# Loading q and k into attention: one transfer per half of a row block, over 128 partitions, in place of one per token half, over 64

## What is computed

```python
xn = _layernorm(x)
# graph part: mean over incoming edges of edge_attr (106250 edges, sorted by dst), then an MLP
agg = segment_sum(edge_attr, dst) / max(count, 1)
g   = xn + relu(concat([xn, agg]) @ W1 + b1) @ W2 + b2
# attention part: 8 heads of 64, q and k through a sigmoid, flow normalizers over all tokens
q, k, v = split(xn @ W_qkv.T + b_qkv)          # q, k = sigmoid(q), sigmoid(k)
i, o, i_hat, o_hat = ...                       # sums of q and k over the tokens
vw = v * softmax(o_hat, over tokens)
kv = einsum('bshd,bshe->bsde', k, vw)          # per token: 64 x 64, summed over the 8 heads
r  = einsum('bshd,bsde->bshe', q / i, kv) * sigmoid(i_hat)
x  = x + g + r.reshape(...) @ W_out.T + b_out
# expert part: one expert for all tokens, picked from their mean
x  = x + gate * (layernorm(x) @ We[idx] + be[idx])
```

## Time and profile before

| | |
|---|---|
| median of 3 runs | 2133.06 us (2132.67 to 2135.23) |
| the profiled execution, its own time | 2125.06 us |
| its span, first to last instruction | 2123.3 us |
| PE busy / mean granted clock | 89% / 0.920 |
| POOL, DVE, ACT busy | 63%, 58%, 26% |
| DMA: packets, bytes, mean rate | 502384, 400.77 MB, 189 GB/s |
| hardware queue 1 / software queue 0, share of the 16 engines | 60.2% / 21.8% |
| attention: first load issued, last matmul begins | 1096.93 us, 1575.84 us |

### The profile page before, as it was taken

How to read it: one execution, slowest core, us unless ns; L and a number is a source line. 1 busy time by engine, 2 the same in 40 slices (tenths; PEclk the granted TensorE clock), 3 DMA queues, 4 the chain that set the end, 5 groups by cost and what they waited for, 6 DMA issues and landing times. The chain is left out here.

```text
span 2123.3 us, 31099 instructions
## 1 busy us (share of the span) xinstructions
PE 1884.5 (89%) x10776; PEld 1515.4 (71%) x10776; DVE 1226.6 (58%) x3872; ACT 561.9 (26%) x1314; POOL 1330.5 (63%) x850
## 2 busy tenths in 40 slices
PE   2799999999999999788776989889867999998798
PEld 1688888888888888544435767767755888886686
DVE  3644453443543432277845656666648888885575
ACT  1422333223332223111122121222223434333210
POOL 4888888888888888688888878887886000000100
PEclk9999999999999999866596898989888999999899
DMA  9977887777787777798699999999969776653884
GB/s 286 227 152 146 149 164 149 157 148 139 156 157 152 138 138 138 183 233 204 143 313 184 213 186 218 184 215 194 209 130 249 220 216 209 211 182 118 299 292 151
DMA packets 502384, 400.77 MB, mean 189 GB/s; under 512 B 356932, under 2 KB 369476, under 8 KB 502228
## 3 DMA queue, kind: packets, MB, share of 16 engines
q1 hardware_dynamic: 380164, 369.74, 60.2%
q0 software_dynamic: 119952, 28.99, 21.8%
q10 hardware_dynamic: 2112, 0.07, 0.1%
HBM read 244.05 MB, written 154.62 MB: 188 GB/s over the span
## 5 line engine op out<-in xcount | busy, mean ns | idle before, releaser
L297 POOL DMA_INDIRECT table<-edge_ring,edge_row x831 | 1318.7, 1587 | 305.8 <-issue 228.6
L237 DVE SCALAR_TENSOR_TENSOR edge_sel<-edge_dst_all,edge_dst_f,upper 128x128 f32<-128x128 int16 x831 | 318.0, 439 | 92.7 <-PE edge_sum L249 74.6
L365 PE MATMUL pr_out_bank<-pr_norm_xT_hi,pr_w_hi 128*128 128x512 f32 (+1 forms) x832 | 327.5, 394 | 0.0
L249 PEld LDWEIGHTS edge_sum<-edge_attr,edge_sel 128*128 128x128 f32 x1662 | 241.0, 216 | 109.8 <-DVE edge_sel L237 78.9
L365 PE MATMUL pr_out_bank<-pr_norm_xT_lo,pr_w_hi 128*128 128x512 f32 (+1 forms) x832 | 319.3, 384 | 0.0
L365 PE MATMUL pr_out_bank<-pr_norm_xT_hi,pr_w_lo 128*128 128x512 f32 (+1 forms) x832 | 318.5, 383 | 0.0
L249 PE MATMUL edge_sum<-edge_attr,edge_sel 128*128 128x65 f32 x1662 | 251.5, 301 | 71.1 <-DVE edge_sel L237 70.5
L262 ACT ACTIVATE edge_ring<-edge_sum 128x260 f32<-128x260 f32 (+1 forms) x209 | 80.6, 386 | 561.0 <-PE edge_sum L249 489.0
L2289 POOL DMA_INDIRECT ex_w_raw<-in_w_exp,ex_row x4 | 5.9, 1486 | 335.6 <-issue 335.6
L365 PEld LDWEIGHTS pr_out_bank<-pr_norm_xT_lo,pr_w_hi 128*128 128x128 f32 x832 | 156.6, 188 | 32.1
L365 PEld LDWEIGHTS pr_out_bank<-pr_norm_xT_hi,pr_w_lo 128*128 128x128 f32 x832 | 157.1, 189 | 28.3
(11 more groups left out here) (206 smaller groups left out, 3220.8 us busy)
## 6 DMA issues: line engine op xcount, KB each, us to landing
edge_dst_all<-dst SPq DMA_DIRECT2D x103, 256.0 KB
edge_attr<-in_edge_attr SPq DMA_DIRECT2D x103, 256.0 KB
qk_halves<-pr_stage SPq DMA_DIRECT2D x48, 512.0 KB
h_pre_T<-pr_stage SPq DMA_DIRECT2D x48, 512.0 KB
gn_pre<-h_pre_T SPq DMA_DIRECT2D x48, 512.0 KB, 6.7
done<-qk_halves SPq DMA_DIRECT2D x16, 1024.0 KB
table<-edge_ring,edge_row POOLq DMA_INDIRECT x831
pr_norm_x<-in_x SPq DMA_DIRECT2D x12, 1024.0 KB
```

The lines of the kernel that those rows point to most:

```text
L237: op = dve.scalar_tensor_tensor(out=self.sel[q][0:rows, j, 0:rows], in0=self.dst_all[k][0:rows, t:t + m * (rows - 1) + 1:m], scalar=self.d ...
L249: mm = pe.matmul(self.p_sum[q][0:rows, j * ECOLS:(j + 1) * ECOLS], self.sel[q][0:rows, j, 0:rows], self.attr[k][0:rows, j0 + j, :], start= ...
L297: pool.indirect_dma_start(self.c.table[t], bass.IndirectOffsetOnAxis(ap=self.row[k][0:rows, j:j + 1], axis=0), self.sums[k][0:rows, j, :], ...
L365: mm = pe.matmul(out, a, c, start=first and i == 0, stop=last and i == n - 1)
```

## The change

`load_qk` still issues four transfers for a block. In a full block each now brings the even or the odd heads of one side for both token halves: 128 partitions, on each one run of 4 KB, again 512 KB. The destination's first dimension is the 128 partitions; the source's dimensions are the two token halves, 64 rows, and the run. The order of the four goes from q, k, q, k to q, q, k, k. In the tail block the four transfers have the shapes and the order that they had. Waits and semaphores are the same.

```diff
         def load_qk(b):
-            for half, r in enumerate([BT // 2, BT // 2] if b < FULL else [TAIL]):
-                for side, dst in enumerate((q[b % 2], kk[b % 2])):
-                    rows = slice(half * HDIM, (half + 1) * HDIM)
-                    if r == HALF:
-                        sp.dma_start(dst[rows, :, :].rearrange("d (x o) t -> d x (o t)", x=2),
-                                     c.qk[side, 2 * b + half, :, :, :].rearrange("(x d) o t -> d x (o t)", x=2)
+            for side, dst in enumerate((q[b % 2], kk[b % 2])):
+                for x in range(2):
+                    rows, chunks = slice(x * HDIM, (x + 1) * HDIM), slice(x * CH, (x + 1) * CH)
+                    if b < FULL:
+                        sp.dma_start(dst[:, chunks, :].rearrange("p o t -> p (o t)"),
+                                     c.qk[side, 2 * b:2 * b + 2, rows, :, :].rearrange("w d o t -> w d (o t)")
                                      ).then_inc(qk_in[b % 2], 16)
                     else:
-                        for x in range(2):
-                            sp.dma_start(dst[rows, x * CH:(x + 1) * CH, 0:r],
-                                         c.qk[side, 2 * b, x * HDIM:(x + 1) * HDIM, :, 0:r]).then_inc(qk_in[b % 2], 16)
+                        sp.dma_start(dst[0:HDIM, chunks, 0:TAIL],
+                                     c.qk[side, 2 * b, rows, :, 0:TAIL]).then_inc(qk_in[b % 2], 16)
```

## The result

| | kernel before | changed kernel |
|---|---|---|
| median | 2132.86 us (2128.69 to 2135.23, 4 runs) | 2529.47 us (2523.39 to 2534.71, 4 runs) |
| profiled execution, its own time | 2125.06 us | 2529.68 us |
| its span | 2123.3 us | 2527.9 us |
| ratio, 95% interval | | 1.1863 [1.1834, 1.1892] |

The changed kernel is 19% slower. In the profiled executions the difference is 404.6 us.

The account below looks back on a forecast made before the run. Attention's blocks were taken to end on DMA transfers, largely q and k. +32 at the start, +312 over 11 blocks and 0 behind gave +344 on 2125.06: 2469, or 2477 as median, range 2390 to 2629.

Parts of the forecast that it names:

- Two engines, the same two: Attention's q and k loads: all four confined to the same two DMA engines by the outermost count of 2; chance 0.82.
- A block of 65 us: Period of a full attention block on two engines: 65 us, the middle of 60 to 71, against 36.6 before.
- a rest: Attention block's time beyond q and k: an average engine's other work, queued on the two engines, 18 to 28.6 us.
- the 42 us for q and k: Time two engines at 25 GB/s each take to move a block's 2.1 MB of q and k.
- Issues cost about 0.6 us each before and after: SyncE's issues of transfers in attention: claimed to cost about 0.6 us each, unchanged by the change.
- The start, +32: Block 0's q and k land 42 - 9.5 = 32 us later on two engines, delaying the start of attention.
- The tail, 0: After attention's last load: compute as before, scatters keep up, GNN start unchanged; 0, at best a few us won.
- 312: Loads for blocks 1 to 11 set attention's pace: 11 x (65 - 36.6) = +312 us.
- Sixteen engines: Rival for the q and k loads: engine count follows SBUF's 128; -35 us, 2098, from 2080 to 2118; chance 0.12.
- Others for each load: Rival: each q and k load gets a different two engines; 2133 to 2145 us; 0.06 together with the no-effect rival.
- doesn't do what it says: Rival: q and k's load rate comes from scatters, not partitions; 2133 us; 0.06 together with the different-engines rival.

Follow-up runs that it names:

- reordered features: Against the changed kernel: q and k features interleaved by head parity when weights are loaded, so 128 rows stand first on both sides; 2081.04 us, ratio 0.9781 to the kernel before.
- 57 rows and 7: Kernel before, each full-block q and k load of 64 rows cut into one of 57 rows and one of 7; 2356.38 us, ratio 1.105.
- 62 rows and 2: Kernel before, each full-block q and k load of 64 rows cut into one of 62 rows and one of 2; 2559.68 us, ratio 1.2046.
- block 0 alone: Kernel before with only block 0's q and k loads in the changed form, all later ones as before; 2157.37 us, ratio 1.0136.

## Why the prediction was right, and what was off

One table over all kernels that change the number of engines, from the trace's packets: q and k of a block from first to last packet (mean of 11 blocks), first packet to first packet of the next (mean of 10), and the difference.

| kernel | engines | q, k in flight, us | block, us | rest, us |
|---|---|---|---|---|
| before | 16 | 11.9 | 37.1 | 25.2 |
| reordered features | 16 | 7.8 | 32.9 | 25.1 |
| q alone changed | 2, 16 | 31.2 | 54.4 | 23.2 |
| 57 rows and 7 | 3 | 32.9 | 55.8 | 22.9 |
| changed | 2 | 46.8 | 70.1 | 23.3 |
| changed, no scatters | 2 | 42.8 | 64.7 | 21.9 |
| 62 rows and 2 | 2 | 49.9 | 73.0 | 23.1 |

**Two engines, the same two.** Right, and shown three ways: the share of 0.13 at 51 GB/s, the 62-row kernel that loses 20% with nothing but its count, and the three-engine kernel between. That all four loads share their engines is in the times too: a load's 128 packets on two engines of its own take 64 x 183 ns = 11.7 us, and q and k were in flight for 46.8, four times that; in the first 20 us of the block shown, with both loads of q issued before them, 1.8 packets are in flight in the mean, not four. And of v's load, which goes to all 16, just 128 of 1024 packets are held back until k has ended: two sixteenths. By the Trainium skill ("DMA: Bandwidth & Descriptors", Why a DMA increments its semaphore by 16) the largest number up to 16 that divides the outermost counts of both sides decides. The runs agree: 2 and 128 gives two engines, 62 gives two, and 57 gives 1.105, which lies where three engines put it.

**A block of 65 us.** The block is q and k's time and a rest, as forecast, and the rest measured 23.3; it stayed between 21.9 and 25.2 in every kernel. That 23 was hit is in part luck, see below. The term that was mis-sized is the 42 us for q and k: I took 25 GB/s an engine over the 22 of the 106-row store, and measured 46.8 us. The 25 is right for engines that have nothing else, 51 GB/s in the stretch above; what I put into the rest alone, and not into q and k's time, is that the scatters' packets take their turns on the same two engines. Without them it was 42.8. The 4.8 us a block, times 11, are 53 us of the miss.

**The rest is not made of what I made it of.** I had v, the mixing rows and the edge loads queue on the two engines, and priced that as an average engine's other work, 18 to 28.6 us. The order is right, as v's last 128 packets and the mixing rows behind them show. But the DMA share is 0.68 in the rest, so an average engine works 15.1 of its 22.28 us (the trace doesn't show the two by themselves); and leaving out the scatters, 10.5 us of that work, took 1.4 us from it. What the prediction had wrong is SyncE: "Issues cost about 0.6 us each before and after". The four issues of q and k hold it for 25.0 us a block (4.5 before), v's for 10.6, the first of the mixing rows' for 16.1 (13.1 before), and in the trace SyncE waits for no other engine for more than 0.3 us in all of these blocks, before or after: its issues follow one on the other (held 354.9 of 368.5 us before, 683.6 of 699.9 after). The means of ten blocks:

| us from one event to the next | before | changed | no scatters |
|---|---|---|---|
| first to last packet of q and k | 12.0 | 46.8 | 42.8 |
| to the end of the mixing rows' first issue | 3.5 | 2.9 | 2.9 |
| to the next block's first issue for q (all other issues) | 16.8 | 15.5 | 14.9 |
| to its first packet | 4.8 | 4.8 | 4.1 |

So the rest is what SyncE has to issue between two blocks' loads, about the same whatever q and k take (with the reordered features alone SyncE waits for PE in it), and a block is q and k's time on their engines plus that. This is read from the traces; no run moved the issues to another queue, and that a full queue is what holds SyncE is argued.

**The start, +32.** From issue to first rearrangement it was 1111.57 - 1096.93 = 14.6 us before and 51.8 after, 37.2 more; block 0's packets of q and k took 51.1 us from first to last, against 13.3. The forecast had 42 - 9.5. The other 3.9 us of the 41.1 come from a first load issued that much later, at 1100.87, by work ahead of all that changed; the first issues of the other kernels scatter as much (1093.30 with block 0 alone). That kernel measured +30.

**The tail, 0.** Right: -2 us. PE's gap ahead of the GNN is 22.10 us (22.98 before), and the scatters, which trailed attention by 53 us, now end with it.

The sum: 32 + 312 became 41 + 365 - 2 = 404.6, and 2469 became 2529.68. Of the miss of 61 us, 53 are q and k's time in the blocks and 5 the same at the start; 4 come from the later first issue, and 2 go back at the tail. It lay inside the range, whose upper end was built from 22 GB/s an engine. That is near the 22.4 measured, but by chance: the 106-row store had no scatters beside it.

**The rivals.** Sixteen engines fell for the change itself, but its price is confirmed by the kernel with reordered features: 4.3 us a block forecast from rows 6 and 7, and 37.1 - 32.9 = 4.2 measured; its -35 was a too careful sum of that gain, -45 was measured (2081.04 beside 2126.35). "Others for each load" and "doesn't do what it says" are excluded by the same runs. The Trainium skill ("SBUF — State Buffer", Door 1: the DMA port swizzle) sees the change as a gain, and for the 128 partitions by themselves the trace agrees: the rate rose from about 220 to 350 GB/s, once the count let it.

## What to carry to other kernels

Before a transfer is reshaped to reach more partitions, read the first dimension of both its sides as the program writes it: the runs here fit the largest number up to 16 that divides both as the number of engines (2 of 128, 62 and 57 rows were tried). A 2 there made q and k take six times as long as the same 128 partitions with 128 rows in front (46.8 us against 7.8), and with 62 rows it was as bad over 64 partitions. If the layout stands in the way, change what row holds which feature when the weights are loaded, or alternate small loads to the two halves of the partitions: that gave 1.4%, with no change of layout, where the new layout gave 2.2%. A queue whose transfers go to two engines also holds the engine that issues, so count what stands behind it, on all its engines, and the packets of other queues on the same two.

## What was not expected of the hardware

- What loads over 64 partitions cost is not fixed. How the two halves follow one another in time decides: a mean packet of 307 ns with 16 in a row to one half, 217 ns with 2, 176 with both halves in every load. That the engines then less often send to the same half at once is argued; the runs show the grain, not its cause.
- Two engines that do nothing but q and k reach 51 GB/s; with scatters beside them 2.1 MB / 46.8 us = 45 GB/s. The 62-row loads on two engines take longer for the same packets, 49.9 us, and those on three 206 ns a packet instead of 183; why was not tried.
- SyncE was held for 21.30 us at two issues that take 0.6 us each in the kernel before. Nothing of its queue moved on the other 14 engines meanwhile, so v, which goes to all 16, came late on all of them.
